# Each store of a unit and each load of x made as two transfers, of the even and of the odd partitions

## The reference

```python
B, F, E = (256, 200, 64)            # r_feature itself is (512, 200, 64), float32
bilinear = jnp.einsum('bie,ied->bid', feature, weight)   # weight: (200, 64, 64)
out = jnp.einsum('bid,bjd->bij', bilinear, feature)      # (512, 200, 200)
```

## Time and profile before

| | us |
|---|---|
| median of 3 runs | 319.97 |
| lowest, highest | 318.48, 320.57 |
| the profiled execution | 321.71 |
| its span, first to last instruction | 319.8 |

### The profile page before, as it was taken

The page is one execution under the profiler, slowest core; times in us unless marked ns, Lnnn a source line. Parts: engine busy times, 40 slices in busy tenths (PEclk is TensorE's granted clock), DMA queues, the critical chain, the costliest instruction groups (busy, mean ns, idle before and its releaser), DMA issues.

```text
span 319.8 us, 14475 instructions
## 1 busy us (share of the span) xinstructions
PE 237.7 (74%) x6784; PEld 208.0 (65%) x6784; DVE 151.1 (47%) x176; ACT 128.1 (40%) x177; POOL 2.0 (1%) x5
## 2 busy tenths in 40 slices
PE   0067586799977686889967667699986776899960
PEld 0065585578866576776867557687886776878840
DVE  0043444526745535525646535254764556546650
ACT  1023244333644433424544333344553435453640
POOL 2000000000000000000000000000000000000000
PEclk9997979979999978999999999799998999999996
DMA  7999999958999999987899999897899999687996
GB/s 272 419 423 438 396 392 372 345 206 337 327 388 401 406 409 408 386 328 280 342 349 409 408 406 409 340 362 303 339 353 406 404 408 360 249 322 310 373 408 269
DMA packets 38507, 115.62 MB, mean 362 GB/s; under 512 B 4272, under 2 KB 4272, under 8 KB 38064
## 3 DMA queue, kind: packets, MB, share of 16 engines
q1 hardware_dynamic: 38448, 114.71, 92.3%
HBM read 32.77 MB, written 81.92 MB: 359 GB/s over the span
## 4 chain that ended last, share of the span: by engine, by line
PE 74%; issue 17%; DMA 4%; SPq 1%; ACT 0%; DVE 0%
PE psum L251 48%; PE psum L222 17%; PE psum L268 8%; DMA w_sb<-w_dram 4%; PE psum L234 1%; SPq L135 1%; ACT mixed L304 0%; DVE tile L283 0%
## 5 line engine op out<-in xcount | busy, mean ns | idle before, releaser
L251 PE MATMUL psum<-x_sb,mixed 64*64 64x200 f32 x3072 | 167.5, 351 | 25.9 <-issue 23.9
L251 PEld LDWEIGHTS psum<-x_sb,mixed 64*64 64x64 f32 x3072 | 133.7, 139 | 44.1 <-issue 33.2
L283 DVE COPY tile<-psum 128x800 f32<-128x800 f32 x100 | 99.2, 992 | 106.8 <-PE psum L251 98.2
L283 ACT COPY tile<-psum 128x800 f32<-128x800 f32 x100 | 82.7, 827 | 82.2 <-PE psum L251 62.8
L222 PE MATMUL psum<-x_sb,w_sb 64*64 64x64 f32 x3072 | 65.8, 226 | 41.1 <-issue 24.5
L222 PEld LDWEIGHTS psum<-x_sb,w_sb 64*64 64x64 f32 x3072 | 64.2, 139 | 44.1 <-issue 42.7
L304 ACT COPY mixed<-psum 64x512 f32<-64x512 f32 x48 | 27.8, 580 | 47.5 <-PE psum L222 46.9
L304 DVE COPY mixed<-psum 64x512 f32<-64x512 f32 x48 | 33.1, 689 | 28.1 <-PE psum L222 26.8
L306 ACT COPY mixed<-psum 128x512 f32<-128x512 f32 x24 | 14.1, 587 | 48.1 <-PE psum L222 48.1
L268 PE MATMUL psum<-x_sb,tails 128*32 128x200 f32 x512 | 26.7, 357 | 2.1 <-issue 2.1
L306 DVE COPY mixed<-psum 128x512 f32<-128x512 f32 x24 | 16.6, 691 | 20.1 <-PE psum L222 20.1
## 6 DMA issues: line engine op xcount, KB each, us to landing
out_dram<-tile SPq DMA_DIRECT2D x192, 400.0 KB, 5.7
x_sb<-x_dram SPq DMA_DIRECT2D x64, 400.0 KB, 7.6
w_sb<-w_dram SPq DMA_DIRECT2D x2, 2048.0 KB, 16.4
out_tail_dram<-tile SPq DMA_DIRECT2D x8, 400.0 KB, 4.3
w_sb<-w_dram SPq DMA_DIRECT2D x1, 2304.0 KB, 21.8
```

The costliest lines, as they stand in the source:

```text
L251: last = nc.tensor.matmul(psum[half_rows(pair), n % BANK_PAIRS * 2 + h, a * FIELDS:(a + 1) * FIELDS], mixed[half_rows(h), (CHUNKS * g + c) ...
L283: copy(tile[:, k % SLOTS, engine], psum[:, bank:bank + 2, 0:2 * FIELDS]).then_inc(copied[engine], 1)
```

## The change

Every store of a unit and every load of x is issued as two transfers: the partitions 0, 2, 4, ... first, the partitions 1, 3, 5, ... behind them. Each has 64 rows of 3,200 bytes where the one before had 128. Both add 16 to the same semaphore as before, so all counts that are waited for on these semaphores double. The weights' loads, the order of all work and the buffers stay. The number of transfers goes from 267 (200 stores, 64 loads of x, 3 of weights) to 531.

```diff
-UNIT_STORES = 2 * 16
+STRIPS = 2
+TILE_STORES = 2 * STRIPS * 16
@@ load_part0
-        eng.dma_start(x_sb[:, 2 * (g % 2), quads], x[g, 0, :, quads]).then_inc(part0_loaded[g % 2], 16)
+        for i in range(STRIPS):
+            eng.dma_start(x_sb[i::STRIPS, 2 * (g % 2), quads], x[g, 0, i::STRIPS, quads]).then_inc(
+                part0_loaded[g % 2], 16)
@@ load_part1
-        eng.dma_start(x_sb[:, 1, quads], x[g, 1, :, quads]).then_inc(part1_loaded[p], 16)
+        for i in range(STRIPS):
+            eng.dma_start(x_sb[i::STRIPS, 1, quads], x[g, 1, i::STRIPS, quads]).then_inc(part1_loaded[p], 16)
@@ SyncE, stores
-                    sp.dma_start(to[:, e], tile[:, k % SLOTS, e]).then_inc(slot_out[k % SLOTS], 16)
+                    for i in range(STRIPS):
+                        sp.dma_start(to[i::STRIPS, e], tile[i::STRIPS, k % SLOTS, e]).then_inc(
+                            slot_out[k % SLOTS], 16)
@@ waits
-                pe.wait_ge(part0_loaded[g % 2], 16 * PART0_LOADS * (g // 2 + 1))
+                pe.wait_ge(part0_loaded[g % 2], 16 * STRIPS * PART0_LOADS * (g // 2 + 1))
-                pe.wait_ge(part1_loaded[p], 16 * (g + 1))
+                pe.wait_ge(part1_loaded[p], 16 * STRIPS * (g + 1))
-                    eng.wait_ge(slot_out[k % SLOTS], UNIT_STORES * (k // SLOTS))
+                    eng.wait_ge(slot_out[k % SLOTS], TILE_STORES * (k // SLOTS))
```

More of the change, by code:

```diff
@@ L170, in _ @@
             for s in range(SLOTS):
-                sp.wait_ge(slot_out[s], UNIT_STORES * len(range(s, len(OUT_TILES), SLOTS)))
+                sp.wait_ge(slot_out[s], TILE_STORES * len(range(s, len(OUT_TILES), SLOTS)))
         @block.gpsimd
```

## The result

| | before | after |
|---|---|---|
| median, us | 319.23 (4 runs) | 403.41 (4 runs) |
| lowest, highest | 317.12, 320.57 | 402.67, 404.64 |
| the profiled execution, and its span | 321.71, 319.8 | 403.78, 402.0 |

The changed kernel takes 1.267 times as long, with a 95% interval of 1.260 to 1.273. Some executions of any of these kernels take over 1.5% longer than its fastest one; the ratios in this document leave those out. Forecast was no change, 320.5 us, with a range that ended at 350.

What follows compares the result with a forecast made beforehand. The prediction took the DMA engines to bound some 182 us and TensorE 122 us. From the profiled 321.7, +1.5 (semaphore packets) +0 +0 -1 (instruction packets) gave 322.2, less 1.7 to the median: 320.5 us, range 306 to 350.

Steps and rivals of the forecast that it cites:

- the price of an issue on SyncE: SyncE's queue: 0.48 us per half transfer, six issues 2.9 us a tile, hidden behind 3.0 us of DMA; taken as 0.
- The rival with the right mechanism: SyncE in stretches with loads: issues over 0.50 us make it the bound, +32 us at 0.61, about 340 us; chance 0.10.
- The start: First loads: 16 issues end at 8.4 us, TensorE's start at 16.6 stays; it slips 0.5 us if issues take 0.61.
- Semaphore packets: Full DMA stretches: one more packet per engine and transfer, 8 ns each over 182 transfers, +1.5 us, bound 13 us.
- The fixed part of a transfer: Landing of transfers: about 1.4 us of latency is overlapped by the transfers around it, so more transfers cost 0.
- the rate of the DMA engines: Full stretches stay at 405 to 409 GB/s; the forecast is wrong if the rate changes by over 2%, either way.
- The rival of engines that meet: Stepped partitions make DMA engines share ways into SBUF: 338 us at 10% a packet, some 375 at 25%; chance 0.23.
- Its own sign: In the full stretches the DMA share stays at 1.0 while GB/s fall below 390, if engines meet.
- the sign given for SyncE: If SyncE's issues bind, DMA share and GB/s both fall, and SyncE's waits for copies vanish.
- The rival of instructions let in sooner: TensorE's instruction packets wait behind shorter transfers, most 2 us stops shrink to tenths: 301 to 310 us; chance 0.25.
- the argument that these stops only take the shape of the DMA bound: In 161 us of full DMA, TensorE's instruction stops are not the bound, so shortening them gains nothing there.

Runs made afterwards that it cites:

- m2_stream: Kernel before plus six streams of 6,400-byte rows at SyncE's end: loads, then stores, each whole, even and odd, halves; its time says nothing, stream rates were read.
- e_tile: Changed kernel with a tile's two units stored together, as even and odd partitions, 64 rows of 6,400 bytes, 331 transfers: 323.8 us, 1.014 times the kernel before.
- e_loads: Kernel before with only the loads of x split into even and odd partitions, stores whole: 322.0 us, 1.009 times the kernel before.
- t_tile: Kernel before with whole tiles stored as even and odd partitions, 64 rows of 6,400 bytes, loads whole: 0.988 times the kernel before, median 319.0 us.
- e_pool: Changed kernel with the odd partitions' stores issued by GpSimd, SyncE issuing the rest: 1.035 times the kernel before, runs of 330.0 and 330.5 us.
- m3_rows: Kernel before plus single loads at SyncE's end, each waited for, with different numbers of rows; its time says nothing, the time per issue was read.
- m1_issue: Kernel before plus 60 single transfers of several forms at SyncE's end, each waited for; its time says nothing, the time per issue was read.
- e_few: Changed kernel with half of TensorE's score instructions, same 531 transfers, half of the scores not the ones wanted: 394.5 us against the changed kernel's 403.4.

## Why the prediction was wrong

**The failed step is the price of an issue on SyncE.** The prediction put it "between half (nothing) and the whole again" and took the whole, 0.48 us, from the earlier trace rows. That upper bound had no ground: no row showed a transfer of 64 rows, and a smaller transfer was assumed to cost no more to issue than a larger one. It costs 0.60, and 0.64 with the gap behind it, which the 0.48 had in it: a third more. In a tile with loads SyncE needs 3.85 us where the DMA engines need 3.0, so the issuer that was to hide behind them became the bound. The prediction had named the point where cover is gone, 0.50 us, and it lay 4% from its own value; so near a threshold the price deserved both ends and more than a chance of 0.10.

**The rival with the right mechanism had the wrong size.** It said 340 us, the run said 403. It priced only the 48 tiles with loads. The sum from the rows of after: the first store is issued at 33.8 us (5.5 later than before's 28.3 in the earlier trace rows), 48 tiles with loads at 229.25 - 225.40 = 3.85 make 185, 52 tiles without at 227.97 - 225.40 = 2.57 make 134, the long issues 45, and the last store lands 2.3 us behind the last issue's start at 399.1. Together 400 of 402 us. Left out were the tiles without loads, where the DMA engines needed 2.0 and TensorE, over all tiles, 237.7 / 100 = 2.4 us, and the issues that a packet of instructions stretches. Before, there were 55 issues over 1 us too (27 of them over a packet of instructions; DMA queues were full then), but SyncE had time to lose; a bound that moves to another engine brings its own delays into the time.

**What held.** The start: 16 issues at 0.64 take 10.2 us and TensorE starts at 21.6; the mechanism was given, with 0.5 us for it in place of 5. Semaphore packets: one takes 9 ns by the records of the trace, where 8 was taken; 4,224 more of them are 2.4 us of each DMA engine. The fixed part of a transfer is hidden, as said: in the changed kernel a transfer lands 2.8 us after its issue, and they follow each other at 0.64.

**What held only in the main: the rate of the DMA engines.** The prediction called itself wrong if they changed by over 2%, and their work grew by 5%. Of these 14 us the semaphore packets make 2.4. The 3,200-byte packets make 11.5: their median stays at 126 ns, and their mean goes from 131 to 137, so some of them take far longer. It shows where loads of x run alone, from 3 to 10 us, before and then after (columns as in the earlier trace rows):

```profile
3.00:10.00 7.00, 0.00 (x0) 0.00 (x0) 0.00 (x0) 0.00 (x0) 0.00 (x0) 1.00 1.02 389
```

```profile
3.00:10.00 7.00, 0.00 (x0) 0.00 (x0) 0.00 (x0) 0.00 (x0) 0.00 (x0) 1.00 0.90 277
```

At a full share the first would be 381 GB/s and the second 308; the mean packet takes 133 and 165 ns there. Where stores run alone, from 380 to 400 us after, it takes 127. So the split loads are slower for the DMA engines and the split stores are not, as in m2_stream. With SyncE as the bound this costs the changed kernel little, but it would count where the DMA engines are full; its reason is open.

**The rival of engines that meet** had 0.23 and would have been taken for right by the time alone (25% gave 375). Slower DMA work is there, at 5%, and not at what the time would need. Its own sign, a share of 1.0 with fewer GB/s, isn't there: share and GB/s fall together, the sign given for SyncE. SyncE's waits for copies, which were to vanish, did: the largest row of its waits (us in total, times, longest us) is 87.0 us before and 16.3 after, 10.0 of these before the first store.

```profile
SPq L161 <- ACT tile L283: 87.0, 54, 13.3
```

```profile
SPq L166 <- ACT tile L289: 16.3, 15, 10.0
```

**The rival of instructions let in sooner.** TensorE's stops called "issue" in e_tile are 19.3 + 10.6 + 1.9 + 0.5 = 32 us where they were 24.5 + 23.9 + 2.1 + 2.0 = 52.5 before, and the kernel is no faster. But it is not the split stores that shorten them: e_loads, with whole stores, has 19.6 + 12.8 + 2.3 + 1.3 = 36 us of them, and t_tile, with split stores and whole loads, 29.2 + 17.7 + 3.2 + 2.0 = 52 in its profiled execution, as many as before. So the argument that these stops only take the shape of the DMA bound has support; that smaller transfers shorten them is neither shown nor excluded.

## What to carry to other kernels

Before splitting transfers, write the ledger of the queue that issues them: number of issues times the time of one, per tile, against what the tile takes, and measure that time for the very form; here 64 rows cost 0.60 us in a row where 128 cost 0.44. When DMA share and GB/s fall together, transfers land sooner after their issue and the issuer's instructions follow each other without a pause, look at the issuer for the bound before the DMA engines. Where a split is wanted, give the second issue to a queue with time (e_pool got 73 of the 84 us back), or make the pieces longer, so that the number of issues stays (t_tile).

## What the runs showed of the hardware that was not expected

- An issue on SyncE with nothing queued takes 0.31 us for 16 to 96 rows tried, 0.35 for 128, and 0.47 for exactly 64 (m3_rows; 0.47 to 0.52 in m1_issue); 32 rows take 0.31 as neighbours and 0.47 at a step of two. Why is open.
- Most issues of over 1 us fall together with a packet of TensorE's instructions on the DMA engines, 49 of 50 in the changed kernel, some 0.9 us each; with 12 packets fewer (e_few) there were 12 such issues fewer. With full DMA queues, in the kernel before, it is 27 of 55.
- A stream of stores of one half of the partitions after the other ran at 255 GB/s, of even and odd partitions at 407, as fast as whole ones. Loads of even and odd partitions are slower than whole ones: 325 against 368 GB/s in the streams.
